# A graph network kernel on one core: masks and index turn reordered at the junction of two graphs

## The reference

```python
neigh = (adj_ > 0) & ~eye
rank = jnp.cumsum(ni, axis=-1) - ni
skip = jnp.where(nb > T, (nb + K - 1) // K, 1)
rem = neigh & (sk > 1) & (rank % sk == sk - 1) & mask[:, :, None]
rem = rem | jnp.swapaxes(rem, 1, 2)
nd = jnp.where(rem, 0.0, adj_) > 0
vals = jnp.where(nd[..., None], x[:, None, :, :], jnp.inf)
s = jnp.sort(vals, axis=2)
for tau, w in zip((0.25, 0.5, 0.75), (0.25, 0.5, 0.25)):
    pos = tau * jnp.maximum(nv - 1, 0)
    lo, hi = floor(pos), ceil(pos)
    agg = agg + w * (v_lo + frac * (v_hi - v_lo))
out = x + agg
y = (relu(out @ W1 + b1) @ W2 + b2) * mask
x = layernorm(x + y)
```

## Time and profile before

| | |
|---|---|
| median of 3 runs | 3867.75 us (3863.54 to 3868.38) |
| the profiled execution | 3872.41 us, its span 3870.6 us |
| mean granted TensorE clock | 0.811 |
| VectorE busy | 3180.9 us (82%) |
| TensorE busy | 2635.5 us (68%) |
| ScalarE busy | 1949.1 us (50%) |
| VectorE's waits: L1386 on lookups L580 | 219.5 us in 150 waits |
| DMA queue of SP | 154.49 MB, 23.8% of 16 engines |

### The profile page before, as it was taken

One profiled execution on the slowest core, in us unless ns is written; L12 is line 12 of the kernel. 1 busy time (PEld: TensorE's weight loads), 2 busy tenths in 40 slices (PEclk: granted clock), 3 DMA queues, 4 the chain that ended last, 5 costly groups with the idle time before them and its releaser, 6 DMA issues. The chain is left out here.

```text
span 3870.6 us, 48616 instructions
## 1 busy us (share of the span) xinstructions
PE 2635.5 (68%) x16944; PEld 1215.1 (31%) x17098; DVE 3180.9 (82%) x5858; ACT 1949.1 (50%) x2672; POOL 8.0 (0%) x21
## 2 busy tenths in 40 slices
PE   0000155777777877778777778787878787887897
PEld 0000022333333333333333333333323333333665
DVE  8999988888888888787878787878888887855676
ACT  2114444565656565656565646565656565553232
POOL 0000000000000000000000000000000000000000
PEclk6555576898889888888898989888989898887777
DMA  1001001323232323222232323232322222332111
GB/s 36 0 14 46 0 11 22 57 40 56 35 57 37 55 38 56 37 54 39 52 42 50 50 41 57 33 59 35 56 43 48 45 49 44 40 56 39 44 33 33
DMA packets 242849, 158.50 MB, mean 41 GB/s; under 512 B 126504, under 2 KB 228026, under 8 KB 242362
## 3 DMA queue, kind: packets, MB, share of 16 engines
q1 hardware_dynamic: 238490, 154.49, 23.8%
q10 hardware_dynamic: 4128, 1.05, 0.2%
HBM read 40.14 MB, written 14.70 MB: 14 GB/s over the span
## 5 line engine op out<-in xcount | busy, mean ns | idle before, releaser
L1002 ACT ACTIVATE hot<-bcast,consts 128x1024 bf16<-128x1024 f32 x744 | 829.8, 1115 | 487.4 <-PE bcast L567 486.8
L1386 DVE SCALAR_TENSOR_TENSOR prod<-near,consts,rows 128x512 f32<-128x512 bf16 x768 | 566.5, 746 | 323.1 <-PE rows L580 219.5
L580 PE MATMUL rows<-hot,table 128*64 128x512 bf16 x4608 | 729.6, 428 | 115.0 <-DVE prod L1386 103.8
L554 PE MATMUL ring<-member,neigh_t 128*128 128x512 bf16 x1924 | 516.3, 407 | 179.4 <-ACT words L963 149.1
L589 PE MATMUL found_bank<-prod,consts 128*64 128x512 f32 x1536 | 446.3, 656 | 3.9 <-DVE prod L1386 3.9
L567 PE MATMUL bcast<-idx_t,consts 32*128 32x512 f16 x1488 | 315.4, 421 | 171.6 <-ACT hot L1002 158.3
L580 PEld LDWEIGHTS rows<-hot,table 128*64 128x64 bf16 x4608 | 225.9, 116 | 408.8 <-issue 320.4
L554 PEld LDWEIGHTS ring<-member,neigh_t 128*128 128x128 bf16 x2048 | 182.6, 103 | 527.7 <-ACT words L963 193.6
L492 PE MATMUL ring<-identb,adj_b 128*128 128x128 bf16 x256 | 35.6, 272 | 380.1 <-ACT adj_b L890 367.5
L567 PEld LDWEIGHTS bcast<-idx_t,consts 32*128 32x128 f16 x1488 | 71.0, 92 | 540.3 <-ACT hot L1002 364.6
L963 ACT ACTIVATE words<-ring 128x512 uint16<-128x512 f32 x256 | 146.5, 592 | 146.8 <-PE ring L554 146.0
(11 more groups left out here) (332 smaller groups left out, 4371.5 us busy)
## 6 DMA issues: line engine op xcount, KB each, us to landing
near<-idx_bt SPq DMA_DIRECT2D x768, 128.0 KB
late<-in_adj_dram SPq DMA_DIRECT2D x16, 1024.0 KB, 5.6
adjt_d<-late SPq DMA_DIRECT2D x16, 512.0 KB, 2.8
adj_l<-adjt_d SPq DMA_DIRECT2D x16, 512.0 KB, 5.6
adj_s<-adjt_d SPq DMA_DIRECT2D x16, 512.0 KB, 3.5
parts_d<-parts SPq DMA_DIRECT2D x6, 512.0 KB, 5.1
table<-parts_d SPq DMA_DIRECT2D x192, 16.0 KB, 2.2
out_dram<-x_all SPq DMA_DIRECT2D x4, 512.0 KB, 3.8
```

The lines of the kernel that those rows point to most:

```text
L554: ins = mm(ring[u % 2][:, :], kept_t[:, j, P * i:P * i + P], member[:, j, n // 2, 512 * (n % 2):512 * (n % 2) + 512], start=(j == 0), stop ...
L580: ins = mm(rows[u % 2][C * h:C * h + C, :], table[:, s, GROUPS * h + g8, :], hot[:, u % HOT, h, :], start=(s == 0), stop=(s == 2))
L1002: run(hot[:, u % HOT].rearrange(flat), spread_bank(l, u)[0][:, 0:2, :].rearrange(flat), ACT.Relu, bias=eq_bias[:, :]).then_inc(S["hot_read ...
L1386: stt(out=prod[:, u % DEEP, :], in0=near[:, u % NEAR, :], scalar=iota_b[:, :], in1=rows[u % 2][:, :], op0=ALU.is_equal, op1=ALU.mult).then ...
```

## The change

It does five things.

1. TensorE: `turn_idx` no longer ends with the wait for all copies, and comes ahead of the products of the next graph's tile 1. Behind it only products 0 and 1 are issued, then comes the wait. ScalarE copies these two behind the index copies.
2. Products 2 and 3 of tile 1 move into `select`, between the first spread and the second.
3. ScalarE makes the three masks of tile 0 at the end of `region`, behind the copies of tile 0's products and ahead of `keep_sum`. The masks of tile 1 move behind `keep_sums` of tile 0.
4. TensorE in `select`: units 2 and 3 go ahead of the two sums of tile 0 (`LEAD[1]` is 4), and ScalarE's one-hot tiles accordingly.
5. `STEP`: most entries grow by one or two, so units come earlier in `region`, with fewer at its end; and VectorE's second `pop` moves behind `gcn_start`.

```diff
-STEP = [LATE + n for n in (0, 1, 2, 4, 5, 6, 8, 10, 12, 13, 14, 16, 18, 19, 21, 23)]
+STEP = [LATE + n for n in (0, 2, 3, 5, 7, 8, 10, 12, 14, 15, 16, 18, 20, 21, 22, 23)]
...
                     ins.then_inc(S["idxT_ps"], 1)
-                pe.wait_ge(S["idxT_ev"], TURNS * b + TURNS)
...
                 if l is not None:
                     spread(l, 0)
+                else:
+                    chunk(b, 1, 0)
+                    chunk(b, 1, 1)
+                chunk(b, 1, 2)
+                chunk(b, 1, 3)
+                if l is not None:
                     spread(l, 1)
-                    units(l, 2)
-                if not b:
-                    for n in range(4):
-                        chunk(b, 1, n)
+                units(l, 2)
                 chunk(b, 1, 4)
+                units(l, 3)
                 chunk(b, 1, 5)
+                units(l, LEAD[1])
                 sum_first(b, 0)
                 sum_size(b, 0)
-                units(l, 3)
                 chunk(b, 1, 6)
-                units(l, LEAD[1])
                 chunk(b, 1, 7)
...
-                if p is not None:
-                    for n in range(4):
-                        chunk(p, 1, n)
                 if t is not None:
                     turn_idx(t)
+                if p is not None:
+                    chunk(p, 1, 0)
+                    chunk(p, 1, 1)
+                if t is not None:
+                    pe.wait_ge(S["idxT_ev"], TURNS * t + TURNS)
...
                 units(l, 3)
-                for i in range(2):
-                    for k in range(TAUS):
-                        mask(b, i, k)
                 chunk(b, 1, 2)
                 chunk(b, 1, 3)
+                units(l, 4)
                 chunk(b, 1, 4)
-                units(l, 4)
+                units(l, 5)
                 chunk(b, 1, 5)
+                units(l, 6)
                 keep_sums(b, 0)
+                for k in range(TAUS):
+                    mask(b, 1, k)
                 chunk(b, 1, 6)
-                units(l, 5)
                 chunk(b, 1, 7)
-                units(l, 6)
...
                             tag(p, 0)
+                    for k in range(TAUS):
+                        mask(p, 0, k)
                 if l is not None:
                     keep_sum(l, d)
-                if p is not None:
-                    chunk(p, 1, 0)
-                    chunk(p, 1, 1)
...
+                if p is not None:
+                    chunk(p, 1, 0)
+                    chunk(p, 1, 1)
...
-                if t_of is not None:
-                    pop(wl, x2, x4, x8, t)
                 units(l, STEP[5])
                 if d is not None:
                     gcn_start(d)
+                if t_of is not None:
+                    pop(wl, x2, x4, x8, t)
```

More of the change, by code:

```diff
@@ L1129, in _ @@
                     tag(0, 0)
+            for k in range(TAUS):
+                mask(0, 0, k)
             for b in range(B):
```

## The result

The changed kernel takes **3906.64 us** (median of 4 runs, 3903.41 to 3911.28) where the kernel before took 3868.07 beside it: a ratio of 1.0103, with a 95% interval of 1.0086 to 1.0121. It is slower, by 38.6 us. 3848 had been forecast and the range ended at 3890.

The account below looks back on a forecast made before the run. VectorE (82% busy) and TensorE (68%) were neither full; waits on ScalarE's masks stood out, then a ScalarE-TensorE chain set the pace. 15 x 3.4 gained less 14 x 2.2 lost is 20 us: median 3848, range 3795 to 3890.

Parts of the forecast that it names:

- Masks ahead: Junction (one graph's choice mixed with the previous graph's lookups): early tile-0 masks remove VectorE's 9.15 us wait at no cost.
- Turn, products, units at the junction: Junction: TensorE and ScalarE walked forward; turn gains 0.4, sums 2.3, tile 2's masks 4.1, net 3.4 us per junction.
- a sign of being wrong: Junction: a granted clock of 0.50 past the first lookup would show the forecast wrong.
- a third of 2.2: Junction: a clock fall while TensorE stands during tile 1's masks could cost 2.2 us; a third, 0.7, was taken.
- Near and r1: Units behind tile 3: r1 waits 0.9 us for TensorE; near rows, 4.6 after issue, make r6 wait 2.2, r7 0.9.
- The step that failed: Units from r8 on, behind tile 3: order unchanged, fewer units at the end, no waits expected; priced at nothing.
- the forecast's other terms: Junction gains 3.4 us, 15 times; moved units behind tile 3 lose 2.2 us in 14 graphs.
- the 1.82 that this saves: Units behind tile 3: bit counts behind the GCN start remove the old r7's wait, booked as 1.8 us gained.
- The slower one: Junction: TensorE stays at 1.2 GHz through the first lookups, costing 3.6 us each, 54 over forecast: 3902; chance 21%.
- Near is in time: r6 and r7: near rows arrive in time, only 0.8 of 3.1 us stays; 3816, or 3788 with full clock; 20%.
- doesn't do what it says: Whole change: time moves from masks to lookups and sums, the rest is eaten among the moved units; 3868; 17%.

Follow-up runs that it names:

- junction alone: Changed kernel with the old STEP and the second pop in its old place: 3818.27 us, ratio 0.9872 to the kernel before.
- masks alone: Kernel before with one edit, tile 0's masks made behind the last copy of tile 0's products: 3865.13 us, ratio 0.9987.
- masks behind: Junction alone, with tile 1's masks made behind the copies of products 6 and 7: 3814.72 us, ratio 0.9861 to the kernel before.
- bit counts back: Changed kernel with the second pop back ahead of the GCN start, STEP still new: 3866.42 us, ratio 0.9996 to the kernel before.
- filler in the mix: Changed kernel plus ten unused 512-column matmuls on TensorE between the first and second rank counts: 3864.58 us, ratio 0.9992 to the kernel before.
- near first: Changed kernel with SP issuing r6's and r7's near rows ahead of the store of the turned adjacency: 3852.31 us, ratio 0.9958 to the kernel before.
- mix alone: Kernel before with only the new STEP and the second pop moved behind the GCN start: 3931.84 us, ratio 1.0167.
- fillers at the turn: Masks behind, plus unused matmuls: six ahead of the index turns, one behind each of the first eight: 3796.45 us, ratio 0.9814 to the kernel before.
- late units moved ahead: Junction alone, with STEP's last entries 20, 22, 23 instead of 19, 21, 23: 3829.23 us, ratio 0.9897 to the kernel before.
- all of it together: Changed kernel with near first, filler in the mix, masks behind and fillers at the turn: 3799.28 us, ratio 0.9816 to the kernel before.
- two repairs: Changed kernel with near first and filler in the mix together: 3813.60 us, ratio 0.9857 to the kernel before.

## Why the prediction was wrong

**Masks ahead: right, with a condition.** L1434's wait went at every junction and nothing behind the masks was late in the changed kernel (in the junction alone the first index copy was). The run with the masks alone shows that it needs more of the junction's change, by its rows the earlier turn: without it the same edit gains 0.1%.

**Turn, products, units at the junction: right up to the first values, too high behind them.** Last turn done 4.4 us after the graph's start (forecast 1762.5 less 1758.06, 4.4; measured 1778.0 less 1773.61). First value at 12.0 and 11.8 (forecast 12 to 13). L1427 waiting 4.07 (3 to 5). The sums of tile 0 were 1.6 earlier (2.3), tile 2's masks 1.6 earlier in most graphs (3.4), tile 3 by 2.5 in most (3.4). The working behind it was a forward walk of two engines at prices from rows. Its one soft place was how long the clock stays low. Behind the turns it rose sooner than I had it (2.87 for the first two products, 3.4 taken). It fell once more, for 3.3 us at 1786.80, around the second and third lookups, which I had named as a sign of being wrong. And behind the stand at tile 1's masks it fell in most graphs and cost some 1.7, where I had taken a third of 2.2.

**Near and r1: right.** I took 4.6 from issue to use; at r6 it was 4.95 (1893.71 less 1888.76), with the store beside it. The DMA formula of the Trainium skill (DMA: Bandwidth & Descriptors, Anatomy of one DMA), by which near would have been in time, is given there for transfers that GpSimd issues, and near is issued by SP, so it did not apply. The last graph's rows had set it aside; the wait of 2.47 bears that out.

**The step that failed** is this: "From r8 on the order is the old one, two units on, and at the end there are fewer between VectorE's index steps, where nothing waited; I price that at nothing." It cost 4.0 us in the graph shown and 3.7 in most, more than everything else in the mix, and turned the sign. With the forecast's other terms, 15 x 3.4 − 14 x (2.2 + 3.7) is a loss of 32 us. A typical graph has 2.5 gained at the junction, 2.2 and 3.7 lost in the mix, 3.4 lost in all: that is 191.1 for 187.7. A second and smaller term was mis-sized too, the 0.7 for the clock at tile 1's masks: of the 1.8 that tile 2's masks are short of the forecast, it has 1.0 and the sums have 0.7. The order was indeed the old one. What was new was that TensorE came early. I wrote of the bit counts behind the GCN start that they "give TensorE time for r8 and r9", and booked the 1.82 that this saves. I did not ask what TensorE does with more time than it needs. It stood for 2.81 us, its granted clock fell to 0.50 (1.2 GHz), and the work that comes in one piece just then, counts, convolution, spread, lookup and totals, was done at half pace while VectorE waited for it. The ten unused matmuls take these waits away (0 and 0.63 are left at r10 and r11), and the total falls by 42 us; the bit counts in their old place do much the same.

**The rivals.** The slower one had the right mechanism, TensorE left at 1.2 GHz ahead of lookups for which VectorE waits, and a fair price (3.6 a graph), but the wrong place: I looked for it only where I had seen a low clock before, at the junction, and there the first lookup ran at full pace (0.84). A low clock is not a property of a stage: a new stand can bring it wherever an edit makes one. Not each does (the 2.81 us at 1922.07 cost nothing), but each such place in the mix should have had its price and its chance. The rule of the Trainium skill (TensorE: Matmul & The Clock Gate, What's actually happening), that activity releases the throttle, agrees with both fillers' windows of 1.00; I had used it at the junction and not in the mix. "Near is in time" and "doesn't do what it says" did not come true.

**Luck in it, too.** Up to tile 3 the junction alone was 3.6 ahead, the total says 3.3, and the forecast was 3.4. But the forecast had all of it at tile 2's masks, and they were only 2.6 ahead, tile 2 itself 2.1. The other 1.5 came between tiles 2 and 3, where the lookup's wait of 1.70 shrank, which the forecast did not have. And the masks behind took 2.9 of waiting from a graph, and the total gained 0.2 a graph. Totals of this kernel, as a later section shows, do not follow small gains, so the agreement of the two totals says little.

## What to carry to other kernels

When an edit gives an engine more time, look for where it will now stand, and if the engine is TensorE, price what comes behind that stand at the lower clock too, as a rival with a chance. Here one stand of 2.81 us cost 3.7 to 4.0, one of 3.33 some 1.7, and another of 2.81 nothing. Look at more than one graph of a trace: the loops of this kernel differ among themselves. Follow an edit to the next point at which all engines meet, also through work whose order it leaves alone, and follow each queue that it passes: SP's near rows stood behind a store that hangs on ScalarE. To find out whether a loss is the clock's, put unused matmuls into the stand; if the time comes back, they are the test and a repair in one.

## What I had not expected of the hardware

**Unused matmuls pay.** Ten of them a graph gave 42 us, 14 at and ahead of the turns 18 us, and the transposes, each four followed by a ScalarE copy, did not bring the clock up by themselves (0.50 through the 5.8 us of the changed kernel's turns, 1.00 with fillers ahead of them and between them; which of the two places does it was not run apart). With the products straight ahead of them, in the kernel before, the turns ran at 1.00 without fillers.

**A graph's time comes in steps.** Most graphs of most kernels take one of three times: 184.3 us (junction alone, masks behind), 187.7 (before, bit counts back, filler in the mix, near first, masks alone), or 191.1 (as changed, mix alone with some at 194.7). The steps are 3.4. Kernels whose graphs differ in waits by several tenths come out on the same step, and most edits here moved the time by a whole step or hardly at all. That fits with the masks behind, which brought 3.6 us in all where their waits had shrunk by 2.9 a graph, and with near first and the filler, whose waits differ in size and whose graphs both take 187.7 (of the 6 us between their profiled executions 5.8 lie in the second graph alone). The stretches at 0.50 stand in nearly the same place of most graphs of a kernel meanwhile (the first behind the turns from 13.0 and 12.4 us on in the two graphs of the changed kernel). Not all graphs keep to the steps: with fillers at the turn there are some of 179.7, 181.2 and 181.6 among those of 184.3, with the late units moved ahead they lie between 184.1 and 186.3, and with all of it together between 182.2 and 184.8. What ties a graph's time to the steps no run here shows, and it stays open; a cost of under 3 us a graph is better read from the waits and windows of a graph than from this kernel's total.

**The sum of two repairs.** Near first and the mix's filler each gave one step and together two (3906.6 to 3813.6, 93 us). The turn's fillers and the masks behind, on top of both, gave 14 us, not another step.
